# Attention with two heads on the row halves of TensorE, three score banks and maxima in pairs

## What is computed

```python
mod = silu(c) @ w_adaln + b_adaln
sh_msa, sc_msa, g_msa, sh_mlp, sc_mlp, g_mlp = split(mod, 6)
h = _modulate(_ln(x), sh_msa, sc_msa)
qkv = (h @ w_qkv + b_qkv).reshape(B, N, 3, nh, hd).transpose(2, 0, 3, 1, 4)
q, k, v = (qkv[0], qkv[1], qkv[2])
attn = softmax(einsum('bhqd,bhkd->bhqk', q, k) * hd ** (-0.5), axis=-1)
o = einsum('bhqk,bhkd->bhqd', attn, v).transpose(0, 2, 1, 3).reshape(B, N, C)
x = x + g_msa[:, None, :] * (o @ w_proj + b_proj)
xf = _modulate(_ln(x), sh_mlp, sc_mlp).reshape(-1, C)
topk_logits, topk_idx = top_k(xf @ w_gate, 2)
gates = softmax(topk_logits)
# the two chosen experts of each token, weighted by gates:
#   gelu(xf @ w1[e] + b1[e]) @ w2[e] + b2[e]
return x + g_mlp[:, None, :] * moe
```

## Time and profile before

| | us |
|---|---|
| three timed runs | 990.72, 993.40, 993.65 (median 993.4) |
| the profiled execution: its time / its span | 992.99 / 991.2 |
| PE busy | 900.9 (91%) |
| DVE busy | 566.0 (57%) |
| ACT busy | 516.8 (52%) |
| POOL busy | 313.3 (32%) |

### The profile page before, as it was taken

How to read it: one execution, slowest core, us unless ns; L and a number is a source line. 1 busy time by engine, 2 the same in 40 slices (tenths; PEclk the granted TensorE clock), 3 DMA queues, 4 the chain that set the end, 5 groups by cost and what they waited for, 6 DMA issues and landing times. The chain is left out here.

```text
span 991.2 us, 15201 instructions
## 1 busy us (share of the span) xinstructions
PE 900.9 (91%) x5111; PEld 639.9 (65%) x5111; DVE 566.0 (57%) x978; ACT 516.8 (52%) x1003; POOL 313.3 (32%) x314
## 2 busy tenths in 40 slices
PE   4878799999999999999999896438999999999995
PEld 3775444454545545555444375328999999999995
DVE  3767658767676776767774068463455444444342
ACT  1531266777776777777778735435443333333331
POOL 3522111012120111111042149626555444444342
PEclk9898799999999999999999969558999999999998
DMA  8051600624216060330631157405332222222221
GB/s 209 10 114 23 129 3 17 131 84 102 64 27 137 17 128 19 74 84 8 153 98 44 35 162 256 149 25 141 84 60 56 44 43 43 36 41 40 43 36 19
DMA packets 59296, 73.99 MB, mean 75 GB/s; under 512 B 24856, under 2 KB 51334, under 8 KB 58200
## 3 DMA queue, kind: packets, MB, share of 16 engines
q1 hardware_dynamic: 50216, 60.32, 24.5%
q0 software_dynamic: 8400, 12.12, 7.3%
q10 hardware_dynamic: 608, 0.59, 0.2%
HBM read 33.87 MB, written 15.73 MB: 50 GB/s over the span
## 5 line engine op out<-in xcount | busy, mean ns | idle before, releaser
L1014 DVE TENSOR_REDUCE negmax<-m_ps 128x1 f32<-128x1024 f32 x256 | 309.2, 1221 | 129.5 <-PE m_ps L1079 128.8
L1001 ACT ACTIVATE probs<-s_ps 128x512 f32<-128x512 f32 x486 | 282.0, 597 | 102.6 <-PE s_ps L1110 79.8
L1110 PE MATMUL s_ps<-stack 96*128 96x512 f32 x486 | 212.4, 444 | 5.4 <-ACT probs L1001 3.6
L1110 PEld LDWEIGHTS s_ps<-stack 96*128 96x128 f32 x486 | 90.7, 189 | 163.0 <-ACT probs L1001 130.3
L1079 PE MATMUL m_ps<-stack 96*128 96x512 f32 x512 | 167.7, 412 | 13.1 <-DVE negmax L1014 7.4
L449 POOL TENSOR_TENSOR parts<-proj_f,parts 128x512 fp32r<-128x512 f32 x32 | 41.0, 1282 | 322.0 <-ACT proj_f L443 322.0
L1124 PE MATMUL o_ps<-probs,v_aug 128*19 128x512 f32 x1024 | 136.1, 604 | 0.5 <-ACT probs L1001 0.5
L1969 PE MATMUL gate_bank<-weights,ht_hi 128*128 x630 | 127.1, 296 | 0.4 <-DVE ht_lo L1865 0.4
L1079 PEld LDWEIGHTS m_ps<-stack 96*128 96x128 f32 x512 | 97.9, 195 | 35.2 <-DVE negmax L1014 16.7
L1945 PE MATMUL h_ps<-weights,xt_hi 128*128 x525 | 115.7, 351 | 4.1 <-DVE xt_hi L1858 4.1
L1691 ACT CAST ht_hi<-ht_ps 128x384 fp32r<-128x384 f32 x105 | 43.5, 488 | 117.4 <-PE ht_ps L1956 117.4
(11 more groups left out here) (213 smaller groups left out, 1111.7 us busy)
## 6 DMA issues: line engine op xcount, KB each, us to landing
stack<-parts SPq DMA_DIRECT2D x96, 256.0 KB, 5.0
w_raw<-in_L_cond_w SPq DMA_DIRECT2D x9, 432.0 KB, 3.6
w_raw<-in_L_cond_w SPq DMA_DIRECT2D x9, 384.0 KB, 3.4
xn_scratch<-h SPq DMA_DIRECT2D x16, 192.0 KB, 3.7
x_in<-in_x SPq DMA_DIRECT2D x4, 576.0 KB, 9.6
o_scratch<-o_norm SPq DMA_DIRECT2D x16, 144.0 KB, 2.4
o_in<-o_scratch SPq DMA_DIRECT2D x16, 144.0 KB, 2.6
xr<-in_x SPq DMA_DIRECT2D x16, 144.0 KB, 3.1
```

What stands on the lines that cost most here:

```text
L1001: nc.scalar.activation(probs[:, st % 2, h], score_bank(g, st, h), ACT.Exp, scale=SCALE)\
L1014: nc.vector.tensor_reduce(negmax[:, half, g % 2, m % 16:m % 16 + 1], m_ps[m % 2][:], AX.X, ALU.max, negate=True).then_inc(max_free, 1)
L1110: nc.tensor.matmul(score_bank(g, st, h), stack[s][:, h, 1, kt // QT, (kt % QT) * P:(kt % QT + 1) * P], stack[s][:, h, 0, half], start=True ...
```

## The change

1. **Row halves.** Heads are taken in pairs. A stack is now 128 rows: head 0 of a pair on rows 0 to 63, head 1 on rows 64 to 127, and the three products without padding on 54 rows, with the two parts of the maxima on rows 54 and 55. Maxima multiply over 54 rows, scores over 56. A pair's two matmuls are issued one behind the other, into different banks. Rows of ones on the keys' side are set once by POOL (`ones_rows`), two stacks in `setup` and the third at the start of attention. A transfer of the stack has 18 rows.
2. **Three stacks** for two, used in turn.
3. **Three score banks in a ring with the projections.** `misc` is gone. Scores and projection units share `s_ps` with three banks (`slot_mm`, `slot_free`; `score_item` and `proj_item` number them). A projection unit has its first four matmuls between the two maxima of its step and its last three behind them. ACT copies it out once (`proj_f`), and POOL makes both the high and the low part.
4. **Maxima in pairs of blocks.** One maximum instruction on DVE still reads 1024 elements a row, but as 512 keys of each of two heads, and gives two numbers. A further small reduction (`rowmax`) joins the two key halves. The transposes of rows and of outputs now take a turn in the two maxima banks.
5. **Order.** On PE a step is: first pair of scores, values, second pair of scores, maxima, (projection,) maxima. `MaxPlan` writes it for all 128 steps: always two maxima a step, rows one step after their half is complete, outputs in steps 10 and 2, projections in steps 1, 4, 7 and 10. The wide banks of the last group are gone. The copy of `o_ps` by ACT stands behind all four exponentials of its step.
6. **SP's order** in a group: projection weights, store, rows of the second half, late weights, store, rows of the next group, and then the stack of the group after it.

```diff
-        self.stacks = [sb(stack, "stack0", [3 * HP, GH, 2, 2, HALF], F32R)]
+        self.stacks = [sb(stack, f"stack{i}", [P, 2, 2, 2, HALF], F32R) for i in range(2)]
...
+    def ones_rows(self, pool, i):
+
+        for hh in range(2):
+            s = slice(hh * self.BLOCK + HP, (hh + 1) * self.BLOCK)
+            pool.memset(f32(self.stacks[i][s, :, 1]), 1.0).then_inc(self.ones_ok, 1)
+            pool.wait_ge(self.ones_ok, 2 * i + hh + 1)
...
     def load_stack(self, sp, g):
-        sp.wait_ge(self.parts_ok, 4 * (g + 1))
-
-        n = HP
+        sp.wait_ge(self.parts_ok, self.parts_count(g, 3))
+        sp.wait_ge(self.ones_ok, 2 * min(g + 1, self.STACKS))
...
+                row = (h % 2) * self.BLOCK + q * HD
+                sp.dma_start(f32(self.stacks[g % self.STACKS][row:row + HD, h // 2]).rearrange("p a b n -> p a (b n)"),
+                             f32(self.parts[h * HP:h * HP + HD, kind]).rearrange("p a b n -> p a (b n)"))\
...
             nc.gpsimd.memset(f32(wqk_lo[:]), 0.0).then_inc(bias_zero, 1)
+            pool.wait_ge(bias_zero, 4)
+            for i in range(2):
+                heads.ones_rows(pool, i)
...
-        s_ps = [pb(ctx, f"s_ps{i}", [P, HALF]) for i in range(2)]
-        m_ps = [pb(ctx, f"m_ps{i}", [P, N]) for i in range(2)]
+        s_ps = [pb(ctx, f"s_ps{i}", [P, HALF]) for i in range(S_BANKS)]
+        m_ps = [pb(ctx, f"m_ps{i}", [P, 2, HALF]) for i in range(2)]
         o_ps = pb(ctx, "o_ps", [P, HALF])
-        misc = pb(ctx, "misc", [P, HALF])
...
             load_w(2)
             load_rows_of_max(0, 0)
+            load_stack(1)
             for g in range(GG):
-                if g + 1 < GG:
-                    load_stack(g + 1)
-                if g == 0:
-                    load_rows_of_max(0, 1)
-                else:
-                    load_rows_of_max(g, 1)
+                load_w(g + 3)
+                if g >= 1:
                     store(g - 1, 1)
+                load_rows_of_max(g, 1)
...
+                store(g, 0)
                 if g + 1 < GG:
                     load_rows_of_max(g + 1, 0)
-                store(g, 0)
+                if g + 2 < GG:
+                    load_stack(g + 2)
...
+            def parts(g, u):
...
+                nc.gpsimd.tensor_copy(heads.parts[:, hi, half], heads.proj_f[:, u % 2]).then_inc(parts_ok, 1)
+                pool.wait_ge(parts_ok, heads.parts_count(g, u) - 1)
+                nc.gpsimd.tensor_tensor(heads.parts[:, lo, half], heads.proj_f[:, u % 2],
+                                        f32(heads.parts[:, hi, half]), ALU.subtract).then_inc(parts_ok, 1)
+
+            heads.ones_rows(pool, 2)
             split_w(1)
...
+                    for h in range(GH):
+                        exponential(g, st, h)
+                    if st == 0 and g >= 1:
+                        out_of_bank(2 * g - 1)
+                    if st == KT:
+                        out_of_bank(2 * g)
...
+            def scores(g, st, j):
+                half, kt, s = st // KT, st % KT, g % heads.STACKS
                 if kt == 0:
-                    pe.wait_ge(rows_ld[half], 32 * (g + 1))
...
+                for hh in range(2):
+                    k = score_item(g, st, 2 * j + hh)
+                    pe.wait_ge(slot_free, k + 1)
+                    r = slice(hh * heads.BLOCK, hh * heads.BLOCK + heads.MAX_ROW + 2)
+                    nc.tensor.matmul(s_ps[k % S_BANKS][:], stack[s][r, j, 1, kt // QT, (kt % QT) * P:(kt % QT + 1) * P],
+                                     stack[s][r, j, 0, half], start=True, stop=True).then_inc(slot_mm, 1)
...
+                for st in range(STEPS):
+                    items = plan.steps[STEPS * g + st]
+                    scores(g, st, 0)
                     if st >= 1:
                         values(g, st - 1)
                     elif g >= 1:
                         values(g - 1, STEPS - 1)
+                    scores(g, st, 1)
+                    for it in items[:1]:
+                        item(*it)
+                    unit = PROJ_AT.index(st) if st in PROJ_AT and g + 2 < GG else None
+                    if unit is not None:
+                        project(g + 2, unit, slice(0, 4))
+                    for it in items[1:]:
+                        item(*it)
+                    if unit is not None:
+                        project(g + 2, unit, slice(4, len(PRODUCTS)))
```

More of the change, by code:

```diff
@@ new lines, with score_item, proj_item, __init__ @@
+BLOCKS = 2 * GH * QT
+PAIR_BLOCKS = 2
+S_BANKS = 3
+AHEAD = 48
+RATE = 4
+PROJ_AT = (1, 4, 7, 10)
+UNITS = len(PROJ_AT)
+def score_item(g, st, h):
+    before = sum(GH * STEPS + UNITS * (i + 2 < GG) for i in range(g))
+    return UNITS + before + GH * st + h + sum(st > at for at in PROJ_AT if g + 2 < GG)
+def proj_item(g, u):
+    return u if g == 1 else score_item(g - 2, PROJ_AT[u], GH - 1) + 1
+class MaxPlan:
+    def __init__(self):
+        self.lead, self.steps, self.last = [], [[] for _ in range(STEPS * GG)], []
+        self.rows_at, self.out_at, self.count, self.block = {}, {}, 0, 0
+        self.maxima(self.lead, BLOCKS)
+        self.turn(self.lead, "rows", 0)
+        self.maxima(self.lead, AHEAD)
+        due = []
+        for t, items in enumerate(self.steps):
+            g, st = t // STEPS, t % STEPS
+            begun = self.block // BLOCKS
+            self.maxima(items, AHEAD + RATE * t + 2)
+            for turn in due:
+                self.turn(items, "rows", turn)
+            if st == KT + 2:
+                self.turn(items, "out", 2 * g)
+            if st == 2 and g >= 1:
+                self.turn(items, "out", 2 * g - 1)
+            self.maxima(items, AHEAD + RATE * (t + 1))
+            due = range(begun, self.block // BLOCKS)
+        self.turn(self.last, "out", 2 * GG - 1)
+    def maxima(self, items, upto):
+        while self.block < min(upto, 2 * GG * BLOCKS):
+            n = PAIR_BLOCKS
+            if self.block + n > upto:
+                break
+            items.append((self.count, "max", self.block // BLOCKS, self.block % BLOCKS, n))
+            self.block, self.count = self.block + n, self.count + 1
+    def turn(self, items, kind, turn):
+        (self.rows_at if kind == "rows" else self.out_at)[turn] = self.count
+        items.append((self.count, kind, turn, 0, 0))
+        self.count += 1
@@ L968, in _ @@
         def _(act):
-            act.sem_inc(exp_free, 2)
-            def out_of_bank(g, half):
-                n = 2 * g + half
-                act.wait_ge(pv_free, 2 + 16 * g + KT * (half + 1))
-                if n >= 2:
-                    act.wait_ge(out_mm, n - 1)
-                nc.scalar.copy(o_sb[:, half], o_ps[:]).then_inc(o_evac, 1)
-            for u in range(4):
-                heads.high(act, 1, u, misc)
-                heads.whole(act, 1, u, misc)
+            act.sem_inc(slot_free, S_BANKS)
@@ L982, in _, with out_of_bank @@
+            def out_of_bank(turn):
+                act.wait_ge(pv_free, 2 + KT * (turn + 1))
+                if turn >= 2:
+                    act.wait_ge(max_mm, plan.out_at[turn - 2] + 1)
+                nc.scalar.copy(o_sb[:, turn % 2], o_ps[:]).then_inc(o_evac, 1)
+            for u in range(UNITS):
+                project(1, u)
             for g in range(GG):
                 for st in range(STEPS):
-                    units = plan(g)[1][st - 1] if st >= 1 else []
-                    for unit in units:
-                        heads.high(act, *unit, misc)
@@ new lines, in maxima @@
+            def maxima(n, turn, first, count):
+                g, half = turn // 2, turn % 2
+                s = g % heads.STACKS
+                pe.wait_ge(max_free, n + 1)
+                for i in range(count):
+                    if half == 0 and (first + i) % (BLOCKS // PAIRS) == 0:
+                        for hh in range(2):
+                            pe.wait_ge(stack_ld[2 * ((first + i) // (BLOCKS // PAIRS)) + hh], 48 * (g + 1))
+                    hh, kh, qt, j = ((first + i) % 2, (first + i) // 2 % 2, (first + i) // 4 % QT,
+                                     (first + i) // (4 * QT))
+                    r = slice(hh * heads.BLOCK, hh * heads.BLOCK + heads.MAX_ROW)
+                    mm = nc.tensor.matmul(m_ps[n % 2][:, i], stack[s][r, j, 0, half, qt * P:(qt + 1) * P], stack[s][r, j, 1, kh],
```

340 lines of the change are left out of this document (139 added, 201 removed).

## The result

The changed kernel takes 952.55 us (median of four runs, 948.63 to 962.55); the kernel before takes 993.46 us (median of four, 990.72 to 993.65). The ratio is 0.961, with a 95% interval of 0.9534 to 0.9685. 962 us and a gain of 31 were forecast; 41 were gained.

A forecast was written before the change was run, and what follows sets the result against it. Attention was taken to be bound by PE's own instruction stream. Its steps summed to 424 us against 457, 33 less, with 2 taken back for transfers and missed starts: 993 - 33 + 2 = 962 us, range 930 to 1005.

The forecast's parts named there:

- The plain step: Attention step without projection or transposes: 2.67 us after the change, against 3.30 before.
- the ring: Plain attention step: values to second scores 0.99, to exponential 0.54, two exponentials 1.09, release 0.05 before next values: 2.67 us.
- The pair: Two heads' matmuls on different row halves: taken at 0.23 us side by side, upper bound 0.46 one after the other.
- Projection steps: Attention steps with a projection unit: 4.40 us, with four new changes of array shape at 0.15 each.
- Steps with transposes and maxima: Attention steps with transposes but no projection: second maxima wait for DVE to finish the first, 3.8 us a step.
- The copy of o_ps: Behind all four exponentials in attention, so the next values wait for it: 0.48 us more, twice a group.
- The start at the lower clock: First steps of attention, run at the lower clock: 5 us added to the sum.
- The 2 us that I took back for transfers: Allowance on the whole time for transfers and missed starts: 2 us off the 33 us gain.
- (a): Rival in attention: changes of array shape cost 0.39 us instead of 0.15; 985 to 1004 us, most likely 990; chance 0.12.
- (b): Rival in attention: pairs run one after the other, 0.46 us each, plain steps 3.03; 1026 us, slower; chance 0.08.
- (c): Rival in attention: PE's granted clock falls, to 0.79 for instance; about 1018 us, slower; chance 0.12.
- (d): Rival: shape changes nearly free (0.05 us), attention block starts early, less waiting; 925 to 945 us; chance 0.13.

The follow-up runs named there:

- one_half: Changed kernel with maxima and scores of all four heads reading the lower row half (heads 0 and 2 computed twice): 1302.0 us.
- max_in_ring: Changed kernel with the first pair of maxima issued between values and the second scores: 966.5 us.
- values_two_behind: Changed kernel with a third buffer of probabilities and values two steps behind the scores, output copy and transposes a step later: 945.6 us.
- all_same_half: Changed kernel with the two matmuls of each pair, maxima and scores alike, reading the same row half: 974.2 us.
- proj_whole: Changed kernel with the seven projection matmuls in one piece behind both pairs of maxima, in projection steps without transposes: 947.7 us.

## Why the prediction was right, point by point

**The plain step.** 2.67 forecast, 2.66 measured, by each link: values to scores 0.98 (0.99), scores to exponential 0.54, two exponentials 1.09, release 0.05. That the ring and not PE or DVE bounds it was argued then, and is shown now by three runs: with 0.92 us more work PE needs only 0.37 more (one_half), a pair moved into the ring costs 0.24 (max_in_ring), and cut open the ring gives a shorter step (values_two_behind). The changed kernel holds a fourth sign: the last steps, which have no maxima at all for PE or DVE, take the same 2.66. What the prediction left out of its list of chains is the three score banks: that chain is 2.60, just 0.06 below the ring.

**The pair.** Its two matmuls start together where no bank is waited for, and pairs stand 0.23 apart; taken at 0.23 and right. Of the first scores of a step the second starts 0.32 later, which the prediction's list of signs did not foresee. The upper bound is right too: one after the other gives plain steps of 3.03.

**Steps with more in them.** Projection steps: 4.40 forecast, 4.54 measured, because a change of shape costs 0.19 and not 0.15. Steps with transposes and maxima: 3.8 forecast, 3.71 measured; PE waits for DVE in them as described:

```profile
173.83 0.65 PE L1145 MATMUL m_ps<-ident,o_sb 128*128 128x128 f32 x4
175.22 0.50 PE L1132 MATMUL m_ps<-stack 54*128 54x512 f32 x2 [0.74 <-DVE negmax L1064]
```

With a projection between: 4.95 forecast, 4.80 and 4.97 measured. The copy of o_ps: 0.48 forecast, 0.57 measured. These errors cancel, which is luck: a group with projections was 54.0 and is 53.97 (167.64 to 221.61); group 6 was 48.2 and is 47.87.

**Where attention is 7 us shorter than forecast** (417.3 for 424). The start at the lower clock was put at 5 us; from the first scores to the second values it is 8.51 where a plain and a projection step at full clock would be 7.20, so 1.3. That is 3.7 of the 7, and it was the term that was mis-sized. Another 1.1 is group 7: of its two steps put at 3.8 the one with the rows has no second maxima to wait with, and takes 2.66. And 1.6 is group 0, which was counted as a full group but has no earlier outputs to copy (0.57) and to transpose (3.71 for 2.66). The half microsecond that is left I can't place.

**Outside the steps.** SP's stack transfers take as long as before, 1.13 us each, though with 144 KB for 256:

```profile
58.65 13.60 SPq L473 DMA_DIRECT2D stack<-parts  x12
```

So time doesn't go by bytes. The Trainium skill (DMA: Bandwidth & Descriptors, "Why a DMA increments its semaphore by 16 and not by 1") has 18 rows on 9 engines, two rows each; by this rule 13.7 us, and the trace agrees: the 8 KB packets of one transfer come in two rounds of 9, some 0.6 us each (60.2 and 60.8 us), in the kernel before in two rounds of 16 (61.0 and 61.7). The memsets take 7.37 us for four (2 each forecast); no later start of the lead shows them. The wait of the lead's first projection was put at 2 us and is 2.97. The 2 us that I took back for transfers were not needed: PE never waits for a stack or a row transfer in attention. They were as much as the lead cost (1.7), so they were right only by chance.

**The rivals.** (a) fell: 0.19 a change against 0.39. (b) fell, and one_half shows that its plain step would have been true in size had the halves not run beside each other, and that (c) would then have come with it. (c) fell in attention, where the clock stays at 1.00 with PE 94% busy; it lives on in the lead, at 0.70 in the window 74 to 109. The mean granted clock of the slowest of the changed kernel's runs (962.55 us) is 0.921, that of the fastest (948.63) 0.942; where in the slowest run it was lost, no profile shows. (d) fell: the changes cost 0.19, not 0.05, and the block's first maxima start at 73.33 for 74.43, a difference that is smaller than what this start moves by between the executions of kernels that are the same up to there (72.5 to 75.9).

Not tested by themselves are the third stack, the third score bank, the maxima in blocks and the split of the parts on POOL: the runs price the side by side, the places of maxima, copy and projection, and SP's order.

## What to carry to other kernels

Before you price a matmul, write down the ring: what waits for what from one step's values to the next, each link from a row. Work outside it is free until it fills the slack (0.55 us here), and the same work inside it costs its whole spacing. Where two engines' steps are as regular as here, read an edit from the single steps and not from the whole time, which carries the clock of other stages. And ask of each large transfer what stands behind it in its queue: here that order alone was worth 85 us.

## What the runs showed of the hardware

- Matmuls on different row halves pass each other: one that stands third in the program started 0.34 us before the second (all_same_half, 189.79 and 190.13). So a semaphore on the last of several matmuls on different halves can't be taken to cover the others without a look at this. In the changed kernel each score has an increment of its own; the two maxima of a pair, one on each half, share that of the second, and in the step shown above they start within 0.01 us of each other (295.29 and 295.30, 295.53 and 295.53).
- A PE that is busy 99% of the time can stand at 1.2 GHz: with 54 and 56 rows on one half alone the granted clock was 0.50 to 0.55, with the same matmuls in pairs on both halves 1.00 at 94% busy, and with 96 rows in one piece 1.00 at 99%. What it is about the one half that does this, these runs don't tell.
- A change between row halves and the full array costs about 0.19 us: two fewer took 0.38 off a step (proj_whole).
